# Small-head attention: where in its loop a piece of the output projection stands

## The reference

```python
x = x + _L3_xcond_ref(_layernorm(x, axis=-1), cond_1024[:, None, :], ctx_1024, ...)

for i in range(NL):                                    # NL, D, H = 6, 128, 16; HD = 8
    xn = _adaln(x, noise_emb, n1_w[i], n1_b[i])
    q, k, v = jnp.split(xn @ qkv_w[i].T, 3, axis=-1)   # 128 keys
    a = _attn(_rope(q), _rope(k), v, src_mask).reshape(B, L, D) @ so_w[i].T
    x = x + a
    xn = _adaln(x, noise_emb, n2_w[i], n2_b[i])
    q, k, v = xn @ cq_w[i].T, context @ ck_w[i].T, context @ cv_w[i].T   # 77 keys
    a = _attn(_rope(q), _rope(k), v, ctx_mask).reshape(B, L, D) @ co_w[i].T
    x = x + a
    ...
```

## Time and profile before

| | |
|---|---|
| median of three runs | 7440.89 us |
| the profiled execution, its own time | 7424.37 us |
| its span, first to last instruction | 7422.5 us |
| mean granted TensorE clock | 0.842 of full speed |
| PE, DVE, ACT, POOL busy | 81%, 65%, 39%, 14% of the span |

### The profile page before, as it was taken

How to read it: one execution, slowest core, us unless ns; L and a number is a source line. 1 busy time by engine, 2 the same in 40 slices (tenths; PEclk the granted TensorE clock), 3 DMA queues, 4 the chain that set the end, 5 groups by cost and what they waited for, 6 DMA issues and landing times. The chain is left out here.

```text
span 7422.5 us, 188919 instructions
## 1 busy us (share of the span) xinstructions
PE 6016.0 (81%) x79720; PEld 4349.7 (59%) x79720; DVE 4805.5 (65%) x16917; ACT 2871.0 (39%) x4943; POOL 1030.7 (14%) x924
## 2 busy tenths in 40 slices
PE   4454558888879788888799699899898998998987
PEld 3343446566556577777577466566566565665665
DVE  6777964554558766666544577576675775775864
ACT  2121124444434411111111166456455554554563
POOL 1113522212110200000000101110110111011101
PEclk7676778999989755555599899899999999998998
DMA  1000000000000000000100000000000000000000
GB/s 34 1 0 3 1 30 1 1 1 1 1 5 2 6 3 3 3 3 3 25 1 1 19 2 2 11 2 2 11 2 5 8 2 7 6 2 11 2 2 15
DMA packets 61226, 44.67 MB, mean 6 GB/s; under 512 B 22521, under 2 KB 56125, under 8 KB 60227
## 3 DMA queue, kind: packets, MB, share of 16 engines
q1 hardware_dynamic: 60355, 32.26, 1.6%
HBM read 30.14 MB, written 2.10 MB: 4 GB/s over the span
## 5 line engine op out<-in xcount | busy, mean ns | idle before, releaser
L267 DVE TENSOR_REDUCE peak<-ps 128x8 f32<-128x1024 f32 (+1 forms) x832 | 817.0, 1024 | 236.5 <-PE ps L189 236.3
L309 ACT ACTIVATE e<-ps,H_lowT_s 128x1024 f32<-128x1024 f32 x384 | 407.0, 1111 | 249.6 <-PE ps L213 249.6
L309 ACT ACTIVATE e<-ps,H_lowT_c 77x1024 f32<-77x1024 f32 x384 | 405.5, 1105 | 251.9 <-PE ps L213 251.9
L227 PEld LDWEIGHTS ps<-e,H_vt 128*32 128x32 f32 (+1 forms) x12288 | 317.5, 111 | 254.4 <-ACT e L309 135.9
L2489 POOL TENSOR_TENSOR H_rstd<-H_veps,neghalf 128x4 f32<-128x4 f32 (+1 forms) x146 | 161.0, 1103 | 2084.4 <-DVE H_veps L2485 2084.4
L227 PE MATMUL ps<-e,H_vt 128*32 128x128 f32 (+1 forms) x12288 | 429.4, 280 | 23.9 <-DVE xs L287 17.7
L213 PE MATMUL ps<-H_qr,H_km 32*128 32x128 f32 (+1 forms) x12288 | 432.6, 277 | 0.0
L213 PEld LDWEIGHTS ps<-H_qr,H_km 32*128 32x128 f32 (+1 forms) x12288 | 409.8, 171 | 14.7 <-issue 1.0
L189 PE MATMUL ps<-H_km,H_qr 32*128 32x512 f32 (+1 forms) x3072 | 401.1, 543 | 0.0
L2187 ACT ACTIVATE F_rz<-F_gsum 128x32 f32<-128x32 f32 x256 | 58.6, 229 | 822.5 <-DVE F_gsum L2125 822.5
L317 ACT ACTIVATE oT<-ps 128x512 f32<-128x512 f32 x416 | 248.5, 597 | 308.9 <-PE ps L227 303.0
(11 more groups left out here) (650 smaller groups left out, 13952.2 us busy)
## 6 DMA issues: line engine op xcount, KB each, us to landing
G_w<-in_L_ffn_w SPq DMA_DIRECT2D x16, 256.0 KB
H_f<-in_L_xcond_f_w SPq DMA_DIRECT2D x12, 256.0 KB
H_nw<-in_L_xcond_n_w SPq DMA_DIRECT2D x21, 128.0 KB, 2.1
A_cond<-in_cond SPq DMA_DIRECT2D x1, 2048.0 KB
out_x<-x_all SPq DMA_DIRECT2D x1, 2048.0 KB, 8.7
ctx_rows<-in_ctx SPq DMA_DIRECT2D x1, 1232.0 KB
D_wq<-in_L_xcond_attn_wq SPq DMA_DIRECT2D x2, 512.0 KB
D_wk<-in_L_xcond_attn_wk SPq DMA_DIRECT2D x2, 512.0 KB
```

What stands on the lines that cost most here:

```text
L227: last = nc.tensor.matmul(ps[PAD_COLS * s:PAD_COLS * (s + 1), FLAT, r * S:(r + 1) * S], vt_of(u)[0:keys, QUAD * r + s, :], e[0:keys, half, ...
L267: last = nc.vector.tensor_reduce(peak[:, HL * half:HL * (half + 1)], view, AX.X, ALU.max, negate=True)
L309: nc.scalar.activation(e[0:keys, half, :], ps[0:keys, AGAIN[half]:AGAIN[half] + 2, :].rearrange("p b t -> p (b t)"), ACT.Exp, bias=low(u) ...
```

## The change

On PE the pieces move from ahead of `again(u)` to behind `flip(u - 1)`. The wait for `shift_ready` that stood before the pieces goes, since `again` has the same wait. On ACT the take-out moves from ahead of the two exponentials to between them; the hook behind the second exponential is numbered 2 now, and the maskings follow it. The take-out for u = 32, behind the loop, stays where it was.

```diff
@@ small_tensor
                     values(u - 1, 0)
                     values(u - 1, 1)
-                if meanwhile:
-                    pe.wait_ge(sem["shift_ready"], first + u + 1)
-                    meanwhile(u)
                 again(u)
                 if u:
                     flip(u - 1)
+                if meanwhile:
+                    meanwhile(u)
@@ small_scalar
                 if meanwhile:
                     meanwhile(u, 0)
                 exponential(u, 0)
+                if meanwhile:
+                    meanwhile(u, 1)
                 exponential(u, 1)
                 if meanwhile:
-                    meanwhile(u, 1)
+                    meanwhile(u, 2)
@@ during of the earlier block
-                            if part == 1 and u % U < 2 and u + U < B:
+                            if part == 2 and u % U < 2 and u + U < B:
@@ during of the decoder, ACT
                                     if part == 0:
                                         if u == B:
                                             take_out(a, PAIRS - 2)
-                                        elif u % 2 == 0 and u >= 4:
+                                    elif part == 1:
+                                        if u % 2 == 0 and u >= 4:
                                             take_out(a, (u - 4) // 2)
```

## The result

The changed kernel took 7524.19 us (median of four runs, 7519.34 to 7536.61) against 7440.27 for the kernel before: a ratio of 1.0112, with a 95% interval of 1.0093 to 1.0131. It is 84 us slower. A second comparison on another occasion gave 7534.00 against 7439.48, 1.0123 (1.0107 to 1.0138), 95 us. The forecast was 7567: its sign is right and the measured time lies in its range, but the loss is only two thirds to three quarters of the 126 us that the sum gave.

What follows compares the result with a forecast made beforehand. PE was taken to lead, its waits deciding. Self 13.1 us and cross 7.9 us, times six layers, gave 126 us on the profiled 7424, so 7550; with the median 16.5 above that, 7567 us, range 7510 to 7640.

Steps and rivals of the forecast that it cites:

- The gain under the exponential: Pieces run beside the first exponential on PE; saving per pair 0.01 and 0.24 us in self, 0.36 and 0.63 in cross.
- The take-out's wait: L197 of even batches waits for ACT's take-out, F being the turn back's start (L235): +0.45 us self, +0.10 cross.
- The addition's wait and DVE: L197 of odd batches waits for the addition, then DVE's statistics, norm, spread delay the peaks: +0.54 us self, +0.55 cross.
- The sum: All waits less savings: 13.1 us per self pass, 7.9 per cross pass, six layers of both, 126 us slower.
- The case without DVE: Peaks start with the scoring's end, odd steps only +0.47 us self and +0.08 cross: 84 us slower, 7525; chance 0.22.
- Faster: At L197 the waits fall away and the pieces fill PE's idle time: 22 us faster, 7419; chance 0.05.
- no change: The waits cost just what the pieces free: 7441 us; chance 0.04.
- falling clock: PE's idle gaps grow and a tenth of the turns run at half clock: 98 us on top, 7665; chance 0.06.
- the mask rows' upper bound: Mask rows run one half after the other, first scoring 0.35 us later: 206 us slower in all, 7647; chance 0.08.
- The rule weighed: Weight loads overlap matmuls only where row groups differ, so weights' matmuls behind the turn back start 0.17 later: 27 us more, 7594.

Runs made afterwards that it cites:

- x6: The change with both waits made needless by order (DVE adds behind the spread, ACT takes out behind the second exponential): 7314.29 us, 0.9849 against the kernel before.
- x7: The change with DVE's row statistics of a pair moved into the next odd batch, addition and both waits kept: 7505.89 us, 1.0085 against the kernel before.
- after_again: The changed kernel itself, run once more beside the other runs: 7534.00 us, 1.0123 against the kernel before.

## Why the prediction was right, and where it was off

**The gain under the exponential: right.** The pieces cost nothing where they stand now; x6 shows it without the waits.

**The take-out's wait: right, a little too small.** For the even turn, the forecast was 5.60 (1.80 + 3.80) in self and 4.78 in cross; 5.66 or 5.76 and 4.82 or 4.91 came. L197 was released when forecast (F + 1.68, forecast F + 1.60 to 1.71), but the scoring followed it 0.38 later, not 0.16 to 0.20: with all four mask rows directly behind L197, the scoring starts 0.23 behind the rows' start (5476.87 to 5477.10), and not 0.01 as behind the released half before. Most of this came back, since the scoring is then 1.03 long instead of 1.23 and the way from it to the next turn back 3.60 instead of 3.80. By turns it is 14 x (0.11 + 0.09) us per layer too little, 17 us in all.

**The addition's wait and DVE: the mechanism right, the size wrong.** This is the step that failed. For the odd turn, the forecast was 5.92 and 5.50; 5.70 and 5.28 came, 0.22 less in both, 13 x 12 x 0.22 = 34 us. Two numbers in the chain were too late. The addition started at F + 1.14 (5481.84 less 5480.70) and not F + 1.29: the weights' matmuls are listed with 0.61 here and not 0.71, and DVE is released 0.03 behind their end and not 0.09. And the peaks start 0.08 before the spread's listed end (5483.92 against 5483.32 + 0.68), while I let them wait for it. From the addition to the end of the spread it is 2.16, as read before (2.15). DVE's own share in cross is close to the forecast: 5.28 less x7's 4.84 is 0.44, where the prediction had 0.55 less 0.08. In self the scoring's listed end (5482.79 + 1.03) lies 0.10 ahead of the peaks' start, so the two chains end together there, and with 5.69 in x7 DVE's chain costs 0.01 by itself, not 0.54 less 0.47.

**The sum.** 126 less 34 plus 17 are 109 us. By medians the difference is 84 and 95, and in the two profiled executions 7526.74 less 7424.37, 102 us. Of these 102, 11 lie ahead of the decoder, whose first scoring comes at 4259.4 before and at 4270.4 after. The earlier block's first turn of the peaks is already late by more (2314.8 and 2328.5), and nothing ahead of it was changed, so these 11 are no part of the price. That leaves 91. From the first turn back of each pass to its last, summed over the twelve passes, it is 104 us more (1950.0 against 1845.7), near the 109. From the first scoring of a pass to its first turn back, it is 10 us less (186.5 against 197.0): there TensorE's clock may stand at half. The 3 us that are left over lie outside these stretches. In the profile before, eleven of the twelve passes began so, in the one after nine. The first self pass (busy time by stretch, before and then after):

```profile
4270.00:4275.00 5.00, 5.00 (x62) 2.94 (x61) 2.71 (x4) 2.45 (x4) 0.00 (x0) 0.50 0.00 0
```
```profile
4281.00:4286.00 5.00, 4.67 (x86) 2.85 (x79) 3.85 (x7) 3.78 (x6) 0.00 (x0) 1.00 0.00 0
```

A self pass that begins at the upper level reaches its first turn back 13.1 us after its first scoring, the others need 15.5 to 16.4. In the second profile of the changed kernel, after_again, it is eleven passes of twelve again, so the change by itself doesn't keep the clock up there; what does is open.

**The rivals.** The case without DVE named 7525 us, which is nearly the measured median. It is right by its number alone, which is luck: x7 shows that DVE's chain does cost 28 us, and the terms around it were off the other way. Faster, no change and falling clock did not occur; nor did the mask rows' upper bound: the scoring did start later, but was shorter by nearly as much (1.03 instead of 1.23). Behind the first turns of a pass the granted clock stayed at its upper level.

**The rule weighed.** By the Trainium skill, TensorE: Matmul & The Clock Gate, section on row and column tiling, the weights' matmuls would have started 0.17 later than the peaks' turn did before, by the prediction's estimate. The trace shows them at 0.50 behind the turn back's start (5480.70 to 5481.20), while that is listed as busy for 0.66, so the measurement stands against that reading of the rule here, as far as modelled ends allow.

## What to carry to other kernels

Work that is moved into an engine's idle time has readers on other engines, and the next instruction in the same queue may be waiting for those readers: look at its waits first, and count the chain from the moved piece through its reader to that instruction. If the chain is longer than the idle time, see, before you move the piece back, whether its readers can come after the other user of the shared bank, so that order does what the wait did. Here, in x6, that turned 1.1 to 1.2% lost into 1.5% won.

## What was not expected of the hardware

Waits that were fulfilled long before may still have shown in the time. Every second even turn of self took 5.76 instead of 5.67, and L173 then followed L197 by 0.23, as in these two rows of PE's timeline after, instead of 0.15 (5476.72 to 5476.87 above):

```profile
5488.09 0.22 PE L197 MATMUL ps<-ident_b,peak_parts 128*128 128x128 bf16 x1 [0.81 <-ACT H_o8T L2759]
5488.32 0.40 PE L173 MATMUL ps<-H_low_s,ones_b 1*128 1x512 bf16 x4
```

These are the batches that begin a group, whose mask rows stand behind four semaphores instead of one (`table_ready`, `peaks_ready`, `masked_a`, `masked_v`) in the printed order. Between these two rows the trace lists two instructions of PE's queue that only wait, 0.05 us each (L2658 and L181, at 5488.1 and 5488.2); the turns of 5.67 don't have them there. Before, they stood in front of the exponential's wait and cost nothing. That the semaphores are the cause is argued from this order, not shown by a run.
